# A transformer decoder block on one core: y turned one slot earlier in the order, k's product in two halves, attention rows two tiles at a time, and both edges of the feed-forward part reordered

## What is computed

```python
x = layernorm(x + L0_attn(x))             # linear attention, then a feed-forward part
x = layernorm(x + L0_xattn(x, ctx, mask)) # 16 heads of 8 features, causal softmax
x = layernorm(x + L0_ffn(x))              # shared + expert product, gate of 7 experts

def xattn(x, enc, mask):
    q, k, v = x @ WQ, enc @ WK, enc @ WV          # split in 16 heads
    scores = where(mask_or_future, -1e9, q @ k.T / sqrt(8))
    return softmax(scores) @ v @ WO
def ffn(x):
    w = top2(softmax(x @ W_gate)); w /= w.sum()
    return x @ W_shared.T + (w0 + w1 parts) * (x @ W_expert.T) + bias
```

## Time and profile before

| what | value |
|---|---|
| median of three runs | 551.51 us (551.32 to 553.45) |
| the profiled execution | 551.02 us, its span 549.3 us |
| TensorE matmuls | 495.5 us busy, 90% of the span |
| VectorE, POOL, ScalarE | 405.0, 372.7 and 354.2 us busy |
| granted TensorE clock | 0.99 of full over the span |
| stage 3 | from about 255 to 530 us, 16 steps |

### The profile page before, as it was taken

How to read it: one execution, slowest core, us unless ns; L and a number is a source line. 1 busy time by engine, 2 the same in 40 slices (tenths; PEclk the granted TensorE clock), 3 DMA queues, 4 the chain that set the end, 5 groups by cost and what they waited for, 6 DMA issues and landing times. The chain is left out here.

```text
span 549.3 us, 23033 instructions
## 1 busy us (share of the span) xinstructions
PE 495.5 (90%) x9328; PEld 369.2 (67%) x9328; DVE 405.0 (74%) x1410; ACT 354.2 (64%) x649; POOL 372.7 (68%) x685
## 2 busy tenths in 40 slices
PE   2899999998999999998799999999999999999870
PEld 1777777775777777775566767767676666767660
DVE  2777777765777677737577888878888888888866
ACT  1566666656777776764866777666776666767641
POOL 6566666645568785642254888887888878888744
PEclk9999999999999999999999999999999999999987
DMA  6630000000000000001110101211012110120001
GB/s 170 173 118 2 3 2 1 4 2 1 2 0 2 1 2 1 2 2 30 32 33 4 50 8 49 51 51 28 28 52 51 51 31 25 51 51 24 23 2 58
DMA packets 24746, 17.44 MB, mean 32 GB/s; under 512 B 2112, under 2 KB 22464, under 8 KB 24640
## 3 DMA queue, kind: packets, MB, share of 16 engines
q1 hardware_dynamic: 24208, 15.90, 10.5%
q10 hardware_dynamic: 432, 0.07, 0.1%
HBM read 11.77 MB, written 4.19 MB: 29 GB/s over the span
## 5 line engine op out<-in xcount | busy, mean ns | idle before, releaser
L793 ACT ACTIVATE gel<-pair 128x1024 f32<-128x1024 f32 x64 | 51.8, 809 | 40.4 <-PE pair L1427 39.3
L786 ACT ACTIVATE gel<-gel,row_scale 128x512 f32<-128x512 f32 x96 | 66.1, 723 | 18.0 <-DVE gel L1070 15.3
L1369 PEld LDWEIGHTS pair<-w,gel 128*128 128x128 f32 x512 | 60.4, 192 | 8.0 <-issue 5.7
L1369 PE MATMUL pair<-w,gel 128*128 128x128 f32 x512 | 62.5, 276 | 1.0 <-ACT gel L719 1.0
L536 POOL TENSOR_SCALAR k_exp<-k_sb,quad_mask 128x512 f32<-128x512 f32 x64 | 43.2, 694 | 26.9 <-ACT k_sb L766 18.1
L1333 PE MATMUL pair<-hT,w 128*128 128x512 f32 x128 | 58.3, 595 | 1.3 <-ACT lev L714 1.3
L1427 PE MATMUL pair<-ident,gel 128*128 128x128 f32 x384 | 55.3, 280 | 1.5 <-ACT gel L786 1.5
L1427 PEld LDWEIGHTS pair<-ident,gel 128*128 128x128 f32 x384 | 43.3, 141 | 18.4 <-issue 13.5
L1057 DVE TENSOR_REDUCE neg_max<-pair 128x16 f32<-128x512 f32 (+1 forms) x48 | 41.0, 854 | 5.5 <-PE pair L1394 5.5
L1394 PE MATMUL pair<-k_exp,qT 32*32 32x128 f32 (+1 forms) x2048 | 44.3, 333 | 0.0
L513 POOL TENSOR_TENSOR X<-X,proj_sb 128x512 f32<-128x512 f32 x16 | 20.4, 1272 | 35.4 <-ACT proj_sb L677 35.4
(11 more groups left out here) (141 smaller groups left out, 1250.4 us busy)
## 6 DMA issues: line engine op xcount, KB each, us to landing
X<-in_x SPq DMA_DIRECT2D x16, 256.0 KB, 3.1
cT<-in_ctx SPq DMA_DIRECT2D x16, 256.0 KB, 3.9
out_rows<-X SPq DMA_DIRECT2D x15, 256.0 KB, 2.6
mask_rows<-in_mask_early SPq DMA_DIRECT2D x16, 128.0 KB, 3.8
w<-in_L_attn_w SPq DMA_DIRECT2D x2, 256.0 KB, 3.4
out_rows<-X SPq DMA_DIRECT2D x2, 128.0 KB, 1.8
w_kv<-in_L_attn_wk SPq DMA_DIRECT2D x1, 64.0 KB, 3.1
w_q<-in_L_attn_wq ACTq DMA_DIRECT2D x1, 64.0 KB, 2.7
```

The lines of the kernel that those rows point to most:

```text
L786: nc.scalar.activation(part, part, ACT.Exp, scale=row_scale[:, n:n + 1])\
L793: nc.scalar.activation(pT[par].rearrange("p (a c) -> p a c", a=2), turned, ACT.Copy)\
L1369: last = nc.tensor.matmul(bank(6 + q)[:, P * t:P * (t + 1)], gel[:, q, f, P * t:P * (t + 1)], w_2[:, f, :], start=(f == 0), stop=(f == NF ...
```

## The change

The change has these parts:

- **Slot 1 and slot 4.** y is no longer turned in slot 1 for group s + 1 but in slot 4 for group s + 2, and ScalarE copies it there. In its place in slot 1 stands the first half of k's product (256 of 512 columns), and the second half stands in front of the closing scores; the whole product stood behind them. The attention rows are turned and copied before the fourth expert tile. v moves to bank 5, and `MOE_BANK` becomes [6, 4, 5, 4].
- **Attention rows by pairs.** Bank 7 holds two tiles, and `xattend` divides two tiles at once: one reciprocal of 32 sums and one product of 256 columns in slots 2 and 4, where there was one of each per tile in every slot. In the last step tiles 3 and 4 stay apart.
- **End of the feed-forward part.** The scores of tile 1 stand in the middle of the last group's down products; VectorE's maximum and subtraction for tiles 0 and 1 stand ahead of its sums of the last two groups; POOL writes the rows y of the last three groups (`rows_a` on POOL); the exponentials have memory of their own (`soft`).
- **Start.** VectorE writes the rows xn of groups 0 and 1; POOL goes on with group 2.

```diff
-MOE_BANK = [5, 6, 4, 5]
+MOE_BANK = [6, 4, 5, 4]
...
+        soft = sb("soft", [P, 3584])
+        s_late = soft[:, 0:1024]
...
             def rows1(g, p):
                 ln_deviation(pool, ln1, g, mv[p], veps, rstd[p])
+                if g < 2:
+                    return
...
+                    if s - 1 < NG - 3:
+                        ln_offset(pool, ln_a, s - 1, mv_b, negm_b, rstd_b[1 - p], offs_b[1 - p])
+                    else:
+                        rows_a(s - 1, rstd_b[1 - p])
...
+            def rows_a(o, rstd):
+
+                pool.wait_ge(ln_a.done, o)
+                nc.gpsimd.tensor_tensor(negm_b[:, :], mv_b[:, :, 0], minus_one[:, :], ALU.mult)\
+                    .then_inc(ln_a.offs, 2)
+                pool.wait_ge(ln_a.rstd, o + 1)
+                pool.wait_ge(ln_a.offs, 2 * o + 2)
+                for t in range(TG):
+                    last = nc.gpsimd.tensor_scalar(X[:, o * TG + t, :], X[:, o * TG + t, :],
+                                                   negm_b[:, t:t + 1], rstd[:, t:t + 1], ALU.add, ALU.mult)
+                last.then_inc(ln_a.done, 1)
...
-                    if t == 0 and exists(s - 2):
-                        collect((s - 2) * TG + TG - 1, TG - 1, p)
+                    if s == 0 and t == 0:
+                        copy_y(1)
                     if t == 0 and exists(prev):
                         act.wait_ge(xatt_xposed, prev + 1)
                         after(act, xproj_done, prev)
                         nc.scalar.activation(attT[:, :], bank(6), ACT.Copy).then_inc(xattT_ready, 1)
-                    if t == 0 and exists(nxt):
-                        copy_y(nxt)
+                    if t == 0 and exists(s - 2):
+                        collect((s - 2) * TG + TG - 1, TG - 1, p)
                     if t == TG - 1 and exists(prev):
...
                         nc.scalar.activation(y2T[:, :], bank(6), ACT.Copy).then_inc(y2T_ready, 1)
+                    if t == TG - 1 and exists(s + 2):
+                        copy_y(s + 2)
...
-            rows_a(NG - 3, 1)
-            act.wait_ge(down_done, NG)
-            phase3(0, 0, slots=(0, 1))
-            rows_a(NG - 2, 0)
-            phase3(0, 0, slots=(2,))
-            rows_a(NG - 1, 1)
-            phase3(0, 0, slots=(3,))
+            phase3(0, 0)
...
             for g in range(2):
                 statistics1(g, g)
+                ln_rows(dve, ln1, g, lambda t: X[:, g * TG + t, :], lambda t: xn[g][:, t, :],
+                        mv[g], rstd[g])
...
+                if s == NG - 1:
+                    future_keys(0, 0)
+                    shift(0, 0)
...
-            def xattend(n, p, t):
+            def xattend(n, p, part):
...
-                nc.vector.reciprocal(rec[:, 0, 0:H], src[:, :, DH]).then_inc(xrec_ready, 1)
+                nc.vector.reciprocal(rec[:, 0, 0:H * count], src[:, :, DH]).then_inc(xrec_ready, count)
...
                         opened_maxima(n + 2)
-                        after(dve, xatt_xposed, s - 1)
-                        xattend(n, p, t)
...
                         shift(n + 2, 1)
-                        xattend(n, p, t)
+                        after(dve, xatt_xposed, s - 1)
+                        xattend(n, p, (0, 1))
...
-                        xattend(n, p, t)
+                        xattend(n, p, (3,) if s == LAST else (2, 3))
...
-            future_keys(0, 0)
-            phase3(-1, 1, slots=(3,))
+            shift(1, 1)
             phase2(NG, 0)
...
+                    if t == 2 and s == NG:
+                        scores_open(1)
+                        scores_close(1)
...
-                after(pe, xatt_ready, n)
+                if n % 2 == 0 or n == NT - 1:
+                    after(pe, xatt_ready, n)
+                first = H * HV * (n % 2)
...
+            def project_k_half(q, half):
+                cols = slice(GW // 2 * half, GW // 2 * (half + 1))
+                return nc.tensor.matmul(bank(5)[:, cols], w_xk[:, :], cT[q][:, cols], start=True, stop=True)
...
-                        after(pe, v2_ready, g)
-                        turn_y(g)
+                        after(pe, k_ready, g)
+                        project_k_half(q, 0)
...
+                    if t == 3 and exists(s + 2):
                         pe.wait_ge(q_ready, g + 1)
-                        project_v(g, q)
+                        turn_y(s + 2)
...
+                    if t == 0 and exists(g):
+                        project_k_half(q, 1).then_inc(xk_done, 1)
                     if exists(s) and t % 2 == 0 and n + 2 < NT:
                         scores_close(n + 2, n + 3)
-                    if t == 0 and exists(g):
-                        pe.wait_ge(ctx_loaded[q], (g - q) * 8 + 16)
-                        after(pe, moe_ready, s * TG - TG)
-                        after(pe, k_ready, g)
-                        project_qk(cT[q], w_xk, bank(5), xk_done)
...
                         for u in range(TG - 1):
+                            if u == 1 and exists(g):
+                                pe.wait_ge(yT_ready, min(s + 3, NG))
```

More of the change, by code:

```diff
@@ L127, in decoder_layer @@
         gel = sb("gel", [P, 2, NF, GW])
-        big = gel[:, :, :, :].rearrange("p q f n -> p (q f n)")
-        s_late = big[:, 0:1024]
-        s_early = [big[:, 1024 + 512 * i:1024 + 512 * (i + 1)] for i in range(2)]
-        pT = [big[:, 2048:3072], big[:, 3072:3584]]
         cT = [sb(f"cT{i}", [P, GW]) for i in range(2)]
@@ L155, in decoder_layer @@
         k_exp = [sb(f"k_exp{i}", [P, HQ, GW]) for i in range(2)]
+        soft = sb("soft", [P, 3584])
+        s_late = soft[:, 0:1024]
+        s_early = [soft[:, 1024 + 512 * i:1024 + 512 * (i + 1)] for i in range(2)]
+        pT = [soft[:, 2048:3072], soft[:, 3072:3584]]
         used = 0
@@ L333, in ln_offset, with ln_rows_pool @@
                 .then_inc(ln.offs, 1)
-        def ln_rows_pool(pool, ln, g, rows, outs, mv, negm, rstd, part=range(TG)):
+        def ln_rows_pool(pool, ln, g, rows, outs, mv, negm, rstd, part=range(TG), others=0):
             after(pool, ln.done, g)
@@ L341, in ln_rows_pool @@
             pool.wait_ge(ln.rstd, g + 1)
-            pool.wait_ge(ln.offs, g + 1)
+            pool.wait_ge(ln.offs, g + 1 - others)
             for t in part:
@@ L775, in copy_v @@
                         v2[q][rows, :, :, h, 0:DH],
-                        bank(first_bank(g, 4))[rows, :].rearrange("p (b i e) -> p b i e", i=HH, e=DH),
+                        bank(first_bank(g, 5))[rows, :].rearrange("p (b i e) -> p b i e", i=HH, e=DH),
                         ACT.Copy)
@@ L1024, in phase2 @@
                                   ln_a.offs, r * 2)
[L1026 removed]
+            def xattend(n, p, part):
                 dve.wait_ge(pv_done, n + 1)
[L1029 to L1030 removed]
+                count = len(part)
+                src = bank(7)[:, H * HV * (part[0] % 2):H * HV * (part[-1] % 2 + 1)] \
+                    .rearrange("p (h e) -> p h e", e=HV)
+                nc.vector.reciprocal(rec[:, 0, 0:H * count], src[:, :, DH]).then_inc(xrec_ready, count)
                 dve.wait_ge(xrec_ready, n + 1)
[L1032 to L1035 removed]
+                nc.vector.tensor_tensor(
+                    att[p][:, part[0]:part[-1] + 1, :].rearrange("p t (h e) -> p (t h) e", e=DH),
+                    src[:, :, 0:DH],
+                    rec[:, 0, 0:H * count].unsqueeze(2).broadcast_to([P, H * count, DH]),
+                    ALU.mult).then_inc(xatt_ready, count)
             def opened_maxima(n):
@@ L1145, in phase3 @@
                     n = s * TG + t
-                    if n == 0:
-                        shift(1, 1)
                     if t == 0 and exists(old):
@@ L1164, in phase3 @@
                         future_keys(s + 1, q)
-                    if t == 2 and exists(s):
-                        xattend(n, p, t)
+                    if t == 2 and s == LAST:
+                        xattend(n, p, (2,))
                     if t == 3 and exists(s + 1):
@@ L1439, in weigh_values @@
                         nc.tensor.matmul(
-                            bank(7)[b * QW:(b + 1) * QW, 0:H * HV],
+                            bank(7)[b * QW:(b + 1) * QW, first:first + H * HV],
                             future[p][:, t // 2, b * QW:(b + 1) * QW],
@@ L1446, in weigh_values @@
                             last = nc.tensor.matmul(
-                                bank(7)[b * QW:(b + 1) * QW, QB * HV * i:QB * HV * (i + 1)],
+                                bank(7)[b * QW:(b + 1) * QW,
+                                        first + QB * HV * i:first + QB * HV * (i + 1)],
                                 pT[1][:, P * i + b * QW:P * i + (b + 1) * QW],
@@ L1474, in project_v @@
                     for h in range(2):
-                        last = nc.tensor.matmul(bank(first_bank(g, 4))[h * S:(h + 1) * S,
+                        last = nc.tensor.matmul(bank(first_bank(g, 5))[h * S:(h + 1) * S,
```

28 lines of the change are left out of this document (11 added, 17 removed).

## The result

The changed kernel takes 554.14 us (median of 11 runs, 552.76 to 556.22) where the kernel before took 552.0 beside it (11 runs): a ratio of 1.0042, 95% interval 1.0028 to 1.0055. So it is slower by 0.4%, a little less than the 0.5% that I called a difference, but outside my range of 545.0 to 553.5, and slower where my 550.3 had it faster. The profiled execution took 556.22 us, the longest of the eleven, with a span of 554.5. Measured again on another occasion it was 554.37 against 551.84, ratio 1.0039 (1.0021 to 1.0058), so this is the kernel and no accident of one measurement.

What follows compares the result with a forecast made beforehand. TensorE, busy 90% of the span, was taken as the bound, gains being its waits or work leaving it. Terms -0.65 - 2.8 + 0.1 + 2.4 - 0.2 + 0.4 = -0.75 from 551.02 gave 550.3 us, range 545 to 553.5.

Steps and rivals of the forecast that it cites:

- the rows repeat from step to step, so one step stands for all: Cross-attention stage: TensorE's timeline over one full step, 17.13 us, was read as standing for all steps.
- T to W: Full step, slot 1's opening scores (T) to slot 3's weighing (W): forecast 9.66 us instead of 9.83.
- TensorE alone would be ready at 9.83 - 0.33 - 0.48, or T+9.0: Before slot 3's weighing: TensorE ready at 9.0 us after slot 1's opening scores, then waiting 0.6 to 0.7 on VectorE.
- the later maximum: Slot 1: VectorE's maximum starts at T+1.24 instead of T+1.12, so the closing scores start about 0.13 us later.
- The merged pair: VectorE's reciprocal and product for two tiles at once: 0.23 us longer, exactly where slot 3's weighing waits.
- W to T: Full step, slot 3's weighing (W) to the next opening scores of slot 1 (T): forecast 7.67 us instead of 7.30.
- the further 0.1 for y: Slot 4: the second expert product uses y's bank and waits for ScalarE's copy of y, 0.1 us more.
- the rival of working fillers: Slot 4: ScalarE copies y2T and y without holding the expert products; W to T 7.35, step 17.01, 546.5 us; chance 0.22.
- The page's rule: VectorE, full steps: first half would give the step the 0.7 us of VectorE time saved; second half speaks against the change.
- The edges: Start and end of the feed-forward part: gains of 0.65 and 2.8 us.
- the last step: VectorE's all the way: later maximum (0.14) and two-tile attention rows (0.23) count in full, +0.4 us.
- The rival that ended slower: Slot 4 becomes ScalarE's: copy of y delays the exponentials by its whole 0.49, step +0.71, 556.4 us; chance 0.11.

Runs made afterwards that it cites:

- e8: Changed kernel with the store of a group's rows issued one step later in SyncE's program: 550.06 us, ratio 0.9970 to the kernel before.
- e4: Changed kernel with attention rows divided one tile at a time again, as before: 552.47 us, ratio 1.0014 to the kernel before.
- e3: Changed kernel with the second half of k's product behind the closing scores instead of in front: 551.44 us, ratio 0.9999 to the kernel before.
- e2: Changed kernel with y2 turned ahead of y in slot 4: 552.95 us, ratio 1.0009 to the kernel before.
- e1: Kernel before with only the change's start and end of the feed-forward part, full steps as before: 548.64 us, ratio 0.9947.
- e7: Changed kernel with 10 of the v product's 16 instructions issued a second time in slot 3: 556.97 us, ratio 1.0098 to the kernel before.
- e14: Changed kernel with 128 more waits, each satisfied at once, at the start of TensorE's program: 564.78 us, ratio 1.0238 to the kernel before.

## Why the prediction was wrong

**What failed is a term that the sum did not have.** The step of the prediction is "the rows repeat from step to step, so one step stands for all", and with it "This holds for steps 2 to 13: 12 times 0.20 = +2.4": it put the pauses of TensorE's instruction stream and the falls of the clock at nothing, on both sides. In the profiled executions the change adds 4.5 us there on top of the regular steps (6.35 less 1.85), 3.0 by the second profile. The rest of the sum, made anew from the profile, is -3.67 (to T1), +0.4 (step 1), 12 x 0.20 = +2.4, -0.04 (step 14), +1.6 (from T15): +0.7. Of this 1.2 is the clock, and gone in e8, where T15 to the end is 35.28 with nothing but the store moved; what is left is -0.5, and my sum was -0.75. With the irregular part it is +5.2, the difference of the two spans. That profile is of the slowest run of the eleven; the medians are 2.1 us apart. And I took the sum off the profiled execution, 551.02, and not off the median, which was 552.0 over eleven runs: 1.0 us of the miss of 3.8. The timeline had shown the signs before: a step of 17.84 among those of 17.13, which I passed over when I wrote that the rows repeat from step to step.

**T to W: the step that failed is "TensorE alone would be ready at 9.83 - 0.33 - 0.48, or T+9.0".** Slot 3's opening scores wait for VectorE's subtraction and start at T+8.99, so that TensorE alone is ready at T+9.79 (e4). I had taken the 0.16 there for ScalarE's, as the row names it. So the wait came before the opening and not before the weighing, where I had 0.6 to 0.7 of it, and the gain of 0.17 did not come. The terms: the closing scores moved by 0.23, not 0.13, and by the half of k that I put in front, not by the later maximum (e3 takes 0.22 of it back; T+1.96 against 1.95 leaves 0.01 for ScalarE's new order). That half takes 0.63 from its start to the closing scores (322.97 to 323.60), where I had 0.48. From the closing scores to the opening VectorE got 0.26 shorter, forecast 0.25. The merged pair ends at T+9.69 and costs 0.04 at W instead of 0.23, since it lies behind the subtraction (e4).

**W to T: right mechanism, half the size.** 0.20 for 0.37. y2T's copy was 0.34 late (forecast 0.39), but the products only 0.15 (forecast 0.25), and the further 0.1 for y was 0.05 at most. e2 gave 7.38; the rival of working fillers had 7.35 there, so the order of the two turns made more than half of the loss.

**The page's rule.** The Trainium skill, Perfetto Trace Analysis, section Optimizing Scalar/DVE Operations, has grouping help "if the engine is saturated", and breaking up help where it is not but leaves bubbles on other engines. Here neither shows: e4 against the changed kernel has the same step of 17.33, because the merged pair is the last thing of VectorE's chain and slot 3 hangs on the subtraction ahead of it.

**The edges** were right (-3.67 for -3.45 in the trace, -2.9 in the time of e1), and so was the last step: its attention rows are turned 0.46 later, for my 0.4, and in e8, whose two turns take 0.44 as before, T15 to the end is 35.28 for 34.86. The other 1.2 us of the profile are the clock. The rival that ended slower (556.4, by ScalarE's slot) gave nearly the profiled time, and was wrong all the same: the exponentials start at W+4.05 for W+3.85, 0.20 late and not 0.84. No rival had the irregular part.

## What to carry to other kernels

Find where the chain that ends a wait starts, and keep that place free: filling a wait that lies ahead of it costs the filler's overhang in every round. Check the releaser that a row names against the ends of all engines named in the code's waits. And compare the lengths of all rounds, not one: where a few of them are longer and their pauses carry "issue", two versions of a kernel differ by more than the work in their code, and a small change can be judged only with that part taken out or shifted on both sides.

## What was not expected of the hardware

The programs come in pieces while they run (74 packets, 1.21 MB on one instruction queue and 32 packets on another, the same before and after), and for TensorE they are not always in time. The first queue is TensorE's, by the counts: 19,056 instructions in its trace and 74 packets, and with e7's 640 more 77 packets. A pause is mostly 0.2 to 1.5 us, often comes back two steps later at the same instruction, and moves with a shift of the program.

The packets show what a pause waits for. The eighteen profiles have 72 pauses over 0.3 us on TensorE behind 255 us that carry "issue", and 71 of them end 1.2 to 1.6 us after a packet of that queue has landed; stretches of that length behind landings make up about 8% of the time. The one of 438.65 has a packet from 436.26 that takes 0.99, the one of 367.71 a packet from 365.32 that takes 0.98. (The 72nd, in e14, stands before slot 3's opening scores of step 1, where TensorE waits for the subtraction otherwise.)

With the store moved away from mask and context the irregular sum fell from 4.9 to 6.4 down to 0.8 us, and from 1.9 to 0.2, and the packets show how. In steps 4, 6, 8, 10 and 12 of the changed kernel, behind the three transfers, the second packet of the step starts at T+8.09, 9.07, 8.61, 9.06 and 8.42; in the same steps of e8 at T+6.85 to 6.90, and in steps 2 and 14 of the changed kernel, where mask and context are not loaded, at T+6.80 and 6.87. Of these five steps, 6, 8 and 10, where it is latest, have a pause over 0.3 us. So transfers at that time make the packet start later; it takes no longer (0.88 to 1.00 us there). They are not all of it: in the changed kernel with 128 waits, the 1.22 us at 394.24 stand where, from 390 to 396, two instruction packets and 0.01 MB of the data queue moved. Its packet starts at 391.65 and takes 1.33, and what made it start so late was not settled.

The granted clock fell to 0.53 once within the steps of the changed kernel, behind a wait of 0.81 and a pause of 0.88 whose ends lie 2.5 us apart. The same pair at 365.24 and 367.71 brought no fall in that execution, while the second profile of the same kernel has 0.72 in 366 to 372. The step with the fall is 3.8 us over the regular one, the step with the same pair and no fall 1.1. The clock goes with a part of the spread of the eleven runs: those at 0.990 took 552.8 and the one at 0.978 took 556.2, but the seven at 0.984 lie between 553.2 and 555.9. When such a pair brings the clock down stays open.
